# A recurrent layer that spreads B and C two steps ahead, and context attentions with reordered starts

## The reference

```python
def step(h, ts):
    dt, B_t, C_t, x_t = ts
    dA = jnp.exp(A[None] * dt[:, :, None])
    dBx = dt[:, :, None] * B_t[:, None, :] * x_t[:, :, None]
    h = dA * h + dBx
    y = jnp.einsum('bdn,bn->bd', h, C_t) + D * x_t
    return (h, y)
```

```python
q = (xn @ Wq + bq) / sqrt(8)
k = ctx @ Wk + bk
v = ctx @ Wv + bv
out = softmax(masked q k^T) @ v
x = x + out @ Wo + bo
```

## Time and profile before

| | |
|---|---|
| median of 3 runs | 2761.79 us (2755.1 to 2763.84) |
| profiled execution, its own time | 2755.07 us |
| its span in the trace | 2753.3 us |
| PE busy | 2156.3 us (78%) |
| DVE busy | 1703.3 us (62%) |
| ACT busy | 1022.7 us (37%) |
| POOL busy | 494.3 us (18%) |

### The profile page before, as it was taken

The page is one execution under the profiler, slowest core; times in us unless marked ns, Lnnn a source line. Parts: engine busy times, 40 slices in busy tenths (PEclk is TensorE's granted clock), DMA queues, the critical chain, the costliest instruction groups (busy, mean ns, idle before and its releaser), DMA issues. The chain is left out here.

```text
span 2753.3 us, 35561 instructions
## 1 busy us (share of the span) xinstructions
PE 2156.3 (78%) x11954; PEld 1414.4 (51%) x11954; DVE 1703.3 (62%) x4082; ACT 1022.7 (37%) x2225; POOL 494.3 (18%) x843
## 2 busy tenths in 40 slices
PE   6796999967996966356666499489479969888888
PEld 3453888844554534122222255278333427666777
DVE  5465677755763656877776545455668945655655
ACT  2253222212663532433332134422147734433333
POOL 0241111011112310244444222010101100000000
PEclk8597999986986988778888589599779979999979
DMA  7320000022113200000000311000321110000000
GB/s 302 88 61 13 1 1 1 1 62 69 47 40 89 55 19 0 0 0 0 0 0 0 118 46 43 0 1 1 111 65 42 39 39 1 0 0 0 0 1 16
DMA packets 60046, 94.41 MB, mean 34 GB/s; under 512 B 11312, under 2 KB 33136, under 8 KB 58736
## 3 DMA queue, kind: packets, MB, share of 16 engines
q1 hardware_dynamic: 29792, 55.57, 6.0%
q0 software_dynamic: 29952, 36.45, 5.4%
q10 hardware_dynamic: 144, 0.39, 0.1%
HBM read 65.63 MB, written 31.29 MB: 35 GB/s over the span
## 5 line engine op out<-in xcount | busy, mean ns | idle before, releaser
L904 DVE TENSOR_REDUCE m<-banks 128x1 f32<-128x512 f32 (+3 forms) x512 | 272.4, 584 | 80.8 <-PE banks L1057 54.4
L1324 DVE TENSOR_REDUCE m<-banks 128x2 f32<-128x308 f32 x384 | 164.4, 475 | 205.6 <-PE banks L1596 118.1
L2416 PEld LDWEIGHTS banks<-w_ffn,eh 128*128 128x128 f32 x2144 | 279.9, 191 | 21.0
L2416 PE MATMUL banks<-w_ffn,eh 128*128 128x128 f32 x2144 | 281.3, 275 | 0.0
L1025 ACT ACTIVATE p<-banks 128x512 f32<-128x512 f32 (+3 forms) x512 | 233.6, 522 | 97.0 <-PE banks L1103 57.4
L2752 PE MATMUL banks<-hc,w_start 128*128 128x512 f32 x256 | 160.9, 765 | 106.6 <-POOL hc L2696 106.5
L2404 PE MATMUL banks<-x_hi,w_hi 128*128 128x512 f32 x472 | 209.7, 444 | 18.7 <-PEq L330 18.7
L1055 PE MATMUL banks<-K,Qf 32*128 32x512 f32 (+2 forms) x512 | 179.9, 511 | 39.5 <-PEq L330 34.9
L2696 POOL TENSOR_TENSOR hc<-sh,cb 128x1024 f32<-128x1024 f32 x64 | 152.8, 2388 | 197.9 <-ACT cb L2711 153.2
L2405 PE MATMUL banks<-x_lo,w_hi 128*128 128x512 f32 x472 | 188.3, 399 | 0.0
L2406 PE MATMUL banks<-x_hi,w_lo 128*128 128x512 f32 x472 | 187.4, 397 | 0.0
(11 more groups left out here) (397 smaller groups left out, 4386.8 us busy)
## 6 DMA issues: line engine op xcount, KB each, us to landing
Qf<-stack_q_plain POOLq DMA_DIRECT2D x48, 256.0 KB, 3.0
Qf<-stack_q_masked POOLq DMA_DIRECT2D x32, 256.0 KB, 3.0
K<-stack_k_self POOLq DMA_DIRECT2D x32, 256.0 KB, 3.1
w_ffn<-ffn_dram SPq DMA_DIRECT2D x1, 6144.0 KB, 35.6
stack_q_plain<-q_hi SPq DMA_DIRECT2D x24, 256.0 KB, 3.5
stack_q_masked<-q_hi SPq DMA_DIRECT2D x16, 256.0 KB, 3.0
stack_k_self<-k_hi SPq DMA_DIRECT2D x16, 256.0 KB, 3.1
K<-stack_k_ctx POOLq DMA_DIRECT2D x48, 80.0 KB, 2.6
```

What stands on the lines that cost most here:

```text
L904: ins = dve.reduce_max(k.m[:, t, h:h + 1], bank[:, 0:(t + 1) * P if k.kind == "page" else S], AX)
L1324: dve.reduce_max(k.m[:, t:t + 2, h], first_banks[c % 3][:].rearrange("p (a k) -> p a k", a=2)[:, :, 0:S2], AX).then_inc(sem("max_done"), 1)
L2416: last = pe.matmul(bank[:, t * P:(t + 1) * P], k.h[:, n % RING, t * P:(t + 1) * P], w(down.format(e))[:, i * P:(i + 1) * P], start=(i == 0 ...
```

## The change

In `scan_block` each turn of PE's loop spreads unit u+2 in place of u+1, and the exceptions at s = 0 and s = 1 go. In `cross_block` the products with the value bias go. In their place one product bv Wo (the bias given as 128 equal columns) is made once, DVE adds it to the output bias as `k.bo`, and POOL adds that to x. PE takes the batches in the order keys 0, transposes 0, keys 1, queries 0, transposes 1, keys 2, queries 1 and so on. ACT alternates keys and queries of a batch, as do POOL's low parts and SP's stores. The queries use one bank (ps[5], the loop's product bank) instead of two, and the wait for `q_full` of all batches moves from the first scores to the second ones.

```diff
@@ -112,7 +112,7 @@
     "x0_wq": (P, lambda i: i["L0_xattn_wq"].T), "x0_wk": (P, lambda i: i["L0_xattn_wk"].T),
...
     "x0_bq": (1, lambda i: col(i["L0_xattn_bq"])), "x0_bk": (1, lambda i: col(i["L0_xattn_bk"])),
-    "x0_bv": (P, lambda i: row(i["L0_xattn_bv"])), "x0_bo": (P, lambda i: np.broadcast_to(row(i["L0_xattn_bo"]), (P, P))),
+    "x0_bv": (P, lambda i: np.broadcast_to(col(i["L0_xattn_bv"]), (P, P))), "x0_bo": (P, lambda i: np.broadcast_to(row(i["L0_xattn_bo"]), (P, P))),
     "f0_router": (E8, lambda i: i["L0_ffn_router_w"].T),
...
@@ -1223,6 +1223,7 @@
         self.kind, self.masked = kind, kind in ("row", "add")
...
         self.qs = sb("qs", [P, 1])
+        self.bo = sb("bo", [P, P])
         self.full_q, self.full_k = sb("full_q", [P, 2, S]), sb("full_k", [P, 2, KPAD])
@@ -1256,7 +1257,7 @@
     oT = net.xnT_all[:, 0:S]
...
     queries, keys = net.stack_q["masked" if k.masked else "plain"], net.stack_k["ctx"]
-    kv_banks, x_banks, q_banks = (ps[0], ps[1]), (ps[2], ps[7]), (ps[5], ps[6])
+    kv_banks, x_banks, q_bank, bias_bank = (ps[0], ps[1]), (ps[2], ps[7]), ps[5], ps[4]
     mask_rows = {"row": 1, "add": 2, "full": 0}[k.kind]
@@ -1356,6 +1357,8 @@
...
             vector_layernorm_of(dve, ch, net.x, k.n, 0, QT).then_inc(sem("xn_ready"), 1)
+            dve.wait_ge(sem("row_done"), 1)
+            dve.tensor_tensor(k.bo[:], bias_bank[:, 0:P], w(f"{pre}_bo"), ALU.add).then_inc(sem("row_ready"), 1)
             if k.masked:
@@ -1437,13 +1440,13 @@
                 pool.wait_ge(sem("ones_in"), j + 1)
...
             pool.wait_ge(sem("ones_in"), GROUP + 1)
-            for b in range(B):
+            for b in range(B - 1):
                 low_keys(b)
-            low_queries(0)
+                low_queries(b)
+            low_keys(B - 1)
             for n in range(2):
                 load_stacks(n)
-            for b in range(1, B):
-                low_queries(b)
+            low_queries(B - 1)
             for n in range(LAST):
@@ -1451,8 +1454,9 @@
                 if n < B:
...
                         pool.wait_ge(sem("xn_ready"), 2)
+                        pool.wait_ge(sem("row_ready"), 1)
                     x = x_of(net, n)
-                    nc.gpsimd.tensor_tensor(x, x, over(w(f"{pre}_bo"), 1, QT), ALU.add).then_inc(sem("x_biased"), 1)
+                    nc.gpsimd.tensor_tensor(x, x, over(k.bo[:], 1, QT), ALU.add).then_inc(sem("x_biased"), 1)
                     pool.wait_ge(sem("x_biased"), n + 1)
@@ -1509,7 +1512,7 @@
...
                     act.wait_ge(net.stacked_sem[b - 2], stores[b - 2])
-                nc.scalar.activation(k.full_q[:, b % 2], q_banks[b % 2][:], ACT.Identity, scale=scale, bias=k.qs[:]).then_inc(sem("q_full"), 1)
+                nc.scalar.activation(k.full_q[:, b % 2], q_bank[:], ACT.Identity, scale=scale, bias=k.qs[:]).then_inc(sem("q_full"), 1)
                 act.wait_ge(sem("q_full"), b + 1)
@@ -1563,22 +1565,25 @@
                 pe.matmul(bank[:, 0:KPAD], w(f"{pre}_wk"), ctx[:, b, :], start=True, stop=True, skip_group_check=True)
...
                     out = bank[:, KPAD + i * P:KPAD + (i + 1) * P]
-                    pe.matmul(out, part, w(f"{pre}_wv"), start=False, stop=False, skip_group_check=True)
-                    last = pe.matmul(out, w("ones")[0:1, :], w(f"{pre}_bv")[0:1, :], start=False, stop=True, skip_group_check=True)
+                    last = pe.matmul(out, part, w(f"{pre}_wv"), start=False, stop=True, skip_group_check=True)
                 last.then_inc(sem("kv_done"), 1)
-            def normed_queries(b):
-                if b == 0:
-                    pe.wait_ge(sem("xn_ready"), 1)
-                if b == 1:
-                    pe.wait_ge(sem("xn_ready"), 2)
+            def output_bias():
+
+                pe.matmul(bias_bank[:, 0:P], w(f"{pre}_bv"), w(f"{pre}_wo"), start=True, stop=True).then_inc(sem("row_done"), 1)
+
+            def normed(b):
+                pe.wait_ge(sem("xn_ready"), 1 if b == 0 else 2)
                 if b >= 2:
...
                     pe.wait_ge(sem("xnT_ready"), b - 1)
-                    pe.wait_ge(sem("q_full"), b - 1)
                 tensor_transpose_tiles(pe, x_banks[b % 2], k.n.xn[:, b * QT:(b + 1) * QT, :], w("ident")).then_inc(sem("xT_done"), 1)
+
+            def project_queries(b):
                 pe.wait_ge(sem("xnT_ready"), b + 1)
-                pe.matmul(q_banks[b % 2][:], w(f"{pre}_wq"), net.xnT_all[:, b * S:(b + 1) * S], start=True, stop=True).then_inc(sem("q_done"), 1)
+                if b >= 1:
+                    pe.wait_ge(sem("q_full"), b)
+                pe.matmul(q_bank[:], w(f"{pre}_wq"), net.xnT_all[:, b * S:(b + 1) * S], start=True, stop=True).then_inc(sem("q_done"), 1)
@@ -1589,7 +1594,7 @@
                     pe.wait_ge(net.loaded_sem["K"][n % CK], came("K", n, CK))
...
                     pe.wait_ge(sem("zeroed"), 4)
-                    pe.wait_ge(sem("q_full"), B)
+                    pe.wait_ge(sem("row_ready"), 1)
                 if c >= 3:
@@ -1627,6 +1632,8 @@
...
                 bank, j = score_banks[x % 3], u % GROUP
+                if x == 0:
+                    pe.wait_ge(sem("q_full"), B)
                 if u == 0:
@@ -1686,10 +1693,13 @@
                     last = pe.matmul(misc[:, t * P:(t + 1) * P], oT[:, t * P:(t + 1) * P], w(f"{pre}_wo"), start=t == 0, stop=True, skip_group_check=True)
...
+            keys_and_values(0)
+            output_bias()
             for b in range(B):
-                keys_and_values(b)
-            for b in range(B):
-                normed_queries(b)
+                normed(b)
+                if b + 1 < B:
+                    keys_and_values(b + 1)
+                project_queries(b)
             for c in range(nch + FIRST):
@@ -2738,9 +2748,7 @@
             spread(1)
...
                 e, s = divmod(u, NSTATE)
-                if s != 1 and 1 <= u < steps - 1:
-                    spread(u + 1)
-                if s == 0:
+                if u + 2 < steps:
                     spread(u + 2)
```

More of the change, by code:

```diff
@@ L123 @@
     "x1_bq": (1, lambda i: col(i["L1_xattn_bq"])), "x1_bk": (1, lambda i: col(i["L1_xattn_bk"])),
-    "x1_bv": (P, lambda i: row(i["L1_xattn_bv"])), "x1_bo": (P, lambda i: np.broadcast_to(row(i["L1_xattn_bo"]), (P, P))),
+    "x1_bv": (P, lambda i: np.broadcast_to(col(i["L1_xattn_bv"]), (P, P))), "x1_bo": (P, lambda i: np.broadcast_to(row(i["L1_xattn_bo"]), (P, P))),
     "x1_pad": (B * KPAD, lambda i: np.broadcast_to(np.pad(i["mask_Bx1x1xS2_ff0"].reshape(B, S2), ((0, 0), (0, KPAD - S2))).reshape(1, -1), (P, B * KPAD))),
@@ L137 @@
     "x2_bq": (1, lambda i: col(i["L2_xattn_bq"])), "x2_bk": (1, lambda i: col(i["L2_xattn_bk"])),
-    "x2_bv": (P, lambda i: row(i["L2_xattn_bv"])), "x2_bo": (P, lambda i: np.broadcast_to(row(i["L2_xattn_bo"]), (P, P))),
+    "x2_bv": (P, lambda i: np.broadcast_to(col(i["L2_xattn_bv"]), (P, P))), "x2_bo": (P, lambda i: np.broadcast_to(row(i["L2_xattn_bo"]), (P, P))),
     "f2_router": (E8, lambda i: i["L2_ffn_router_w"].T), "f2_router_b": (E8, lambda i: np.broadcast_to(row(i["L2_ffn_router_b"]), (P, E8))),
```

## The result

The changed kernel takes 2660.42 us (median of 4 runs, 2656.64 to 2665.3), the one before beside it 2758.44 (4 runs, 2750.13 to 2763.84). The ratio is 0.9648, interval 0.9617 to 0.9679: about 98 us or 3.5% faster, where 92 were forecast and the median 2669.8.

The account below looks back on a forecast made before the run. No engine is full; waits set the pace: DVE's `dbx` for PE's spread of B (87.7 us), and late `full_q` in the attentions. 2755.1 - 79.5 - 12.5 = 2663; the median, allowing for the profiled run's 6.7 us, 2669.8; range 2647 to 2700.

Parts of the forecast that it names:

- The recurrence: Loop of units: DVE's 87.7 us wait for B goes except 8 at batch starts; gain 79.5 us, bounds 70 and 87.7.
- the prediction's check: Recurrence: each engine's times within a unit against DVE's 3.51 us; DVE should never wait, 3.51 us instead of 5.03.
- a whole unit before DVE wants it: Recurrence: with B of u+2 spread where B of u+1 stood, B is there a whole unit early.
- The three batch starts: Recurrence: DVE still waits for B at each batch start, 2.7 us, three times 8 us; ends 0 and 17.
- the products with D: PE at a batch start in the recurrence: D products run at the low clock, 3.5 us.
- the tail: End of the recurrence: as before, the last y waits for the last hc.
- The rival, that short pauses keep the clock low: Recurrence: PE stays at the low clock and becomes the bound, 45 us lost, 2715, half of it 2692; chance 0.17.
- The slower rival: Recurrence: POOL kept out of the shared port while DVE works, 5.86 us per unit, 2802; chance 0.03.
- The starts: Context attentions: first scores 4.8 us earlier in the first, 3.8 in the others; sum 12.5 us, range 6 to 18.
- the loads behind the low parts of the queries of batch 2: Attention starts: loads issued only 13.6 us after the second norm, landing at 18.2, set the first scores.
- POOL's low part of queries starts 3.52 behind its product: Attention starts: from query product 2 at 8.3 us to POOL's low part at 11.8, taken from old rows.
- The step from one query product to the next: Attention starts: was 3.98 us; with a batch of keys added, about 5.0, so queries 2 start at 8.3.

Follow-up runs that it names:

- scan_only: The kernel before with only the new order of the spreads (u+2 in place of u+1); 0.9684 of the kernel before (0.9653 to 0.9715).
- zeros6_two_ahead: The kernel before with the new order of the spreads and six products of a zero tile per unit on PE; 0.9709 (0.9681 to 0.9738).

## Why the prediction was right, and where not

- **The recurrence, 79.5 us forecast, 85.9 measured.** The chain of the prediction's check holds: DVE doesn't wait, 3.48 us per unit (3.51 taken), hc at 2.35, C in time. One sentence of it does not: B isn't there "a whole unit before DVE wants it". With one bank it can't be, and the check behind that sentence already has it so (not before 4.7, wanted at 7.0, so 2.3 us); measured are 2.2. The three batch starts were put at 2.7 us each and have 1.94 before `dbx` and, in two, 0.8 and 1.0 before the gate, 7.6 against 8. The parts differ: the products with D were put at 3.5 us and take 1.98, at the high clock, while the y ahead of the gate falls to the low one in two of three. What was missed is the tail: I wrote that it is as before, but its y and output projection also run at the high clock now (3.3 us), and a unit is 0.03 us shorter. (87.7 less 8 is 79.7; the 79.5 is a slip that moves nothing.)
- **The role of the clock.** The prediction took it as a rival's price and gave it no share in the gain. In fact it was part of the cause: the fall of the clock in the old kernel's pause made 1.7 of the 3 us of each wait. The sum came out right because it counted the wait whole and not by its parts. The rival, that short pauses keep the clock low, is refuted by the stretch at 0.96; `scan_only` and `zeros6_two_ahead`, with the pauses and with them filled, both have 0.97. The Trainium skill's rule of a clock that goes to and fro with small pauses (TensorE: Matmul & The Clock Gate, "A second HAM failure mode: psum-queue depth-cycling") didn't show within the batches, with pauses of 0.77 and 0.13 us in each unit. It showed at two batch starts, for one y each, behind pauses of 1.39 and 0.34 us.
- **The shared port, in the recurrence.** `dtx` stays at 1.2 us and hc beside it takes 3.19 (1226.84 in the changed kernel). That puts off the y behind it by at most 0.34 us, the pause ahead of y, and the gate waits for that y at two batch starts: less than 1 us, where the prediction had nothing. Whether the fall of the clock in these y hangs on it as well, no run shows; the gate's two waits are 1.9 us together. The slower rival, POOL kept out by a DVE that doesn't pause, has hc at 2.35 us within the batches against it.
- **The shared port, in the starts.** The prediction had no row with POOL first and did not look for the port here. It is in the changed kernel's second norm, on which the start hangs. Alternating the low parts put those of the queries beside it:

```profile
91.01 1.26 POOL L1398 TENSOR_TENSOR q_lo<-full_q,q_hi 128x512 fp32r<-128x512 f32 x1 [7.68 <-ACT q_hi L1517]
...
91.08 1.21 DVE L378 SCALAR_TENSOR_TENSOR rstd<-sq,rstd 128x12 f32<-128x12 f32 x1
...
92.23 0.52 POOL L1391 TENSOR_TENSOR k_lo<-full_k,k_hi 128x160 fp32r<-128x160 f32 x1
...
92.33 0.45 DVE L376 TENSOR_TENSOR sq<-rstd 128x12 f32<-128x12 f32 x1
```

  The same two lines take 0.17 us each elsewhere in this norm. Here each ends within 0.03 us of POOL's instruction, and 1.3 us are lost. The second and third start show the same (1.12 us at 852.25, ending with POOL's low part at 852.05). Before, the low parts of the queries came after the norm, and those of the keys cost it less (0.52 for 0.17 at 88.87). That the instructions end together in all three starts is what the rows show; no run takes the two apart.
- **The starts, 12.5 us forecast, 19 measured.** Up to the first scores 7.4, 6.2 and 6.4 us were gained where 4.8, 3.8 and 3.8 were forecast. The path is the one forecast: the loads behind the low parts of the queries of batch 2 are what the scores wait for. What failed is the size of its terms. In the first attention:

```profile
93.84 3.17 DVE L380 TENSOR_SCALAR xn<-x,aggr,rstd 128x128 f32<-128x128 f32 x12
...
99.36 1.40 PE L1586 MATMUL banks<-xnT_all,w_attn 128*128 128x512 f32 x2
...
103.51 1.12 PE L1586 MATMUL banks<-xnT_all,w_attn 128*128 128x512 f32 x2 [1.60 <-ACT xnT_all L1507]
...
106.08 1.26 POOL L1398 TENSOR_TENSOR q_lo<-full_q,q_hi 128x512 fp32r<-128x512 f32 x1 [2.13 <-ACT q_hi L1517]
```

| term | forecast | measured |
|---|---|---|
| second norm ends later than before, from the start of the block | 0.25 | 1.0 |
| its end to queries 1 | 3.0 | 2.3 |
| queries 1 to queries 2 | 5.0 | 4.2 |
| queries 2 to their low part | 3.5 | 2.6 |
| low parts, up to the loads (107.77) | 1.8 | 1.7 |
| loads to first scores (111.60) | 4.6 | 3.8 |
| sum | 18.2 | 15.6 |

  In two of the terms it is the clock, which the forecast kept low and which rises on the way. "POOL's low part of queries starts 3.52 behind its product" holds a product of 2.07 us, and that takes 1.12 here: its whole miss. "The step from one query product to the next", put at 5.0, is 4.15, since the product takes 1.40 and ACT's batch of keys 0.8 in place of 1.04; ACT sets it, and PE waits 1.60 us for its copy. In the two others it isn't: at the low clock a batch of keys takes 1.39 us (97.97 to 99.36) and not 1.96, and the loads land 0.8 sooner. Against them the norm ends 0.8 later than forecast: `k.bo` took the 0.2 that it was given, and the port the rest, beyond what it cost before. That makes 2.6 us, the difference between 7.4 and 4.8.
- **What the sum hid.** The forecast priced bias and order together and so didn't see that one of the two loses. The rows for it were there: the loads were named as "only then", but I never worked out the start without the new order.
- **Between blocks** the prediction expected no difference; 10 us went the other way in untouched blocks. So part of the closeness of 98 to 92 is luck: by the blocks recurrence and starts gave 13 us more than forecast, and most of that was lost again where nothing was changed.

## What to carry to other kernels

Where an engine with a clock that falls when idle stands in a ring of waits, its pause lengthens its own work: count the ring at both clocks, and look for an order that takes the engine out of the ring before giving it less to do. Filling the pause with empty products is a quick test of how much is clock and how much is order. A profile of one execution can mislead: before a difference of some us between blocks is put down to an edit, compare the granted clock of the blocks, and look at one that no edit touches. And price the parts of a change apart, also where they are made together: a queue that is moved past a load can eat part of what another part gains.

## What was not expected of the hardware

320 empty products on the engine that stood in the ring made the kernel faster (0.9909, interval 0.9874 to 0.9943). The granted clock of a block that no edit touches differs between executions (0.77 to 0.87), and with it its time, by up to 15 us (197.2 to 211.9). DVE instructions of 0.17 us took up to 1.21 us beside a POOL product that had started first, and ended with it. The clock fell twice, for one y each, behind pauses of PE of 1.39 and 0.34 us, where pauses of 0.77 and 0.13 in every unit left it high.
